# Prefix sums of a Mamba-2 block as split fp32r products, with every engine's order written anew

## What is computed

```
zxbcdt = hidden_states @ W_in
z, xBC, dt = jnp.split(zxbcdt, [D_INNER, D_INNER + CONV_DIM], axis=-1)
dt = jax.nn.softplus(dt + dt_bias)
xBC = jax.nn.silu(_causal_conv(xBC, conv_w, conv_b))
a = -jnp.exp(A_log)
y = _ssd(x * dt[..., None], dt * a, B, C)
y = y + x * D[None, None, :, None]
y = y * jax.nn.silu(z)
y = y * jax.lax.rsqrt(jnp.mean(y * y, axis=-1, keepdims=True) + EPS) * rms_w
out = y @ W_out          # then residual and a second layer norm
```

## Time and profile before

| | |
|---|---|
| runs (us) | 782.20, 781.74, 781.94 |
| the profiled execution | 780.59 us, span 778.9 us |
| TensorE clock granted, mean | 0.993 |
| busy: PE, PEld | 748.7 us (96%), 626.4 us (80%) |
| busy: DVE, ACT, POOL | 716.5 us (92%), 675.0 us (87%), 646.7 us (83%) |
| DMA | 20.14 MB, mean 26 GB/s |

### The profile page before, as it was taken

How to read it: one execution, slowest core, us unless ns; L and a number is a source line. 1 busy time by engine, 2 the same in 40 slices (tenths; PEclk the granted TensorE clock), 3 DMA queues, 4 the chain that set the end, 5 groups by cost and what they waited for, 6 DMA issues and landing times. The chain is left out here.

```text
span 778.9 us, 19524 instructions
## 1 busy us (share of the span) xinstructions
PE 748.7 (96%) x5412; PEld 626.4 (80%) x5412; DVE 716.5 (92%) x1594; ACT 675.0 (87%) x1716; POOL 646.7 (83%) x1220
## 2 busy tenths in 40 slices
PE   7799999999999999999999999999999999999983
PEld 6667788878888888888888888888888888888863
DVE  3689899999999999999999999999999999999885
ACT  4988899988898998899898889899889998888873
POOL 5577888988888888888898888888888889887774
PEclk8999999999999999999999999999999999999998
DMA  6000100000000000000000000000000000000000
GB/s 198 2 14 8 35 29 29 15 29 27 13 27 27 17 23 27 15 25 27 27 13 27 27 13 27 27 22 19 27 15 25 27 27 13 27 13 13 1 28 27
DMA packets 21418, 20.14 MB, mean 26 GB/s; under 512 B 2832, under 2 KB 20880, under 8 KB 21392
## 3 DMA queue, kind: packets, MB, share of 16 engines
q1 hardware_dynamic: 20176, 19.82, 7.6%
q10 hardware_dynamic: 1216, 0.02, 0.1%
HBM read 11.45 MB, written 8.39 MB: 25 GB/s over the span
## 5 line engine op out<-in xcount | busy, mean ns | idle before, releaser
L825 DVE SCALAR_TENSOR_TENSOR u<-ring,cw,u 128x256 f32<-128x256 f32 x558 | 260.4, 477 | 9.5 <-ACT u L1393 1.7
L1719 PE MATMUL ring<-xhl,wh 128*128 128x262 f32 x744 | 166.0, 315 | 1.0
L1719 PE MATMUL ring<-wh,xhl 128*128 128x512 f32 (+1 forms) x512 | 158.6, 370 | 1.5 <-DVE u L825 1.0
L1393 ACT ACTIVATE u<-ring,cb,cw 128x256 f32<-128x256 f32 x186 | 106.1, 571 | 51.6 <-PE ring L1719 48.2
L1719 PEld LDWEIGHTS ring<-xhl,wh 128*128 128x128 f32 x744 | 118.4, 189 | 34.5 <-DVE u L825 20.6
L1453 ACT ACTIVATE xdt<-xt_bank,dts 128x64 f32<-128x64 f32 x512 | 111.4, 332 | 0.5 <-PE xt_bank L1799 0.5
L1719 PE MATMUL ring<-xhl,wl 128*128 128x262 f32 x372 | 105.6, 284 | 0.0
L1719 PEld LDWEIGHTS ring<-wh,xhl 128*128 128x128 f32 x512 | 90.1, 188 | 19.3 <-issue 5.1
L847 DVE SCALAR_TENSOR_TENSOR lay<-e_bank,btg 128x512 f32<-128x512 f32 x128 | 87.8, 686 | 15.3 <-ACT e_bank L1436 11.9
L1719 PE MATMUL ring<-wl,xhl 128*128 128x264 f32 (+1 forms) x256 | 86.8, 339 | 0.0
L1436 ACT ACTIVATE e_bank<-e_bank 128x512 f32<-128x512 f32 x128 | 75.4, 589 | 5.7 <-PE e_bank L1824 5.1
(11 more groups left out here) (189 smaller groups left out, 2119.9 us busy)
## 6 DMA issues: line engine op xcount, KB each, us to landing
xin<-in_x_dram SPq DMA_DIRECT2D x32, 256.0 KB, 2.7
out_dram<-obuf SPq DMA_DIRECT2D x31, 256.0 KB, 2.2
lay<-in_w_in_dram SPq DMA_DIRECT2D x1, 776.0 KB, 4.7
lay<-in_w_in_dram SPq DMA_DIRECT2D x1, 512.0 KB, 9.3
wo<-in_w_out_dram SPq DMA_DIRECT2D x1, 512.0 KB, 6.1
lay<-in_f2t_dram SPq DMA_DIRECT2D x1, 256.0 KB, 6.3
lay<-in_f_dram SPq DMA_DIRECT2D x1, 256.0 KB, 8.3
lay<-in_f1t_dram SPq DMA_DIRECT2D x1, 256.0 KB, 8.6
```

Source lines behind the costliest of these rows:

```text
L825: v.scalar_tensor_tensor(out=u[:, ct], in0=conv_bank(k, ct)[:, :, t:t + P], scalar=cw[:, ct, t:t + 1], in1=u[:, ct], op0=ALU.mult, op1=ALU ...
L1393: s.activation(u[:, ct], conv_bank(k, ct)[:, :, HALO:PH], ACT.Identity, bias=cb[:, ct:ct + 1], scale=cw[:, ct, HALO:TAPS]).then_inc(u_done ...
L1719: last = mul(out, a, c, start=first and i == 0, stop=i == n - 1)
```

## The change

1. dt*a is made in three POOL operations in place of one: `a_exact` (128x16), its fp32r copy `a_high` (128x4x16), and the rest `a_low` (same shape). Softplus has steps 0 to 13 and not 0 to 11. ACT's `x_times_dt` waits for dt itself (softplus step 10) and not for the last step.
2. `sums` is six fp32r matmuls in place of three fp32 ones: each of the three products is done with the high and then the low part, added in PSUM. Four POOL operations of 128x128 in the head make the fp32r triangles and the constant columns.
3. `exp_a` moves on ACT from the very front to behind the weight splits, the first branch and five convolution blocks.
4. The order of calls is new on PE, DVE, ACT and POOL, in head, loop and tail. In the loop most of it is a rotation (where the loop turns around), but some calls really move, as shown below.

```diff
-SOFT_STEPS = 2 * LOG_TERMS + 2
+SOFT_STEPS = 2 * LOG_TERMS + 4
...
+            def split_constants():
+                pool.wait_ge(s_gp, 36)
+                g.tensor_copy(upto_r[:, :], upto[:, :])
+                g.tensor_copy(after_r[:, :], after[:, :])
+                g.tensor_copy(a_high[:, :], a_wide[:, :])
+                g.tensor_scalar(a_low[:, :], a_wide[:, :], 0.0, None, ALU.mult).then_inc(s_const, 1)
...
-                        pool.wait_ge(s_an, 2)
-                    shape = [P, QUAD, Q * H]
-                    wide = a_wide[:, :].rearrange("p (r n) -> p r n", r=QUAD)[:, :, 0:Q * H]
-                    g.tensor_tensor(wide, dts[:, b].unsqueeze(1).to_broadcast(shape),
-                                    a_neg[:, :].unsqueeze(1).to_broadcast(shape), ALU.mult).then_inc(a_done, 1)
+                    if i == 2 * LOG_TERMS + 1:
+                        if begun(k - 1):
+                            pool.wait_ge(a_done, k)
+                        else:
+                            pool.wait_ge(s_an, 2)
+                        g.tensor_tensor(a_exact[:, :], dts[:, b], a_neg[:, :], ALU.mult).then_inc(soft, 1)
+                    elif i == 2 * LOG_TERMS + 2:
+                        if begun(k - 1):
+                            pool.wait_ge(sums_in_psum, k)
+                        else:
+                            pool.wait_ge(s_const, 2)
+                        apart(pool)
+                        g.tensor_copy(high, spread).then_inc(soft, 1)
                     else:
+                        g.tensor_tensor(low, spread, high.bitcast(F32), ALU.subtract).then_inc(a_done, 1)
                     return
...
-                act.wait_ge(a_done, k + 1)
+                act.wait_ge(soft, (SOFT_STEPS - 1) * k + 2 * LOG_TERMS + 1)
...
-                mul(bg_bank[:, 0:n], upto[:, :], a_wide[:, 0:n], start=True, stop=True)
-                mul(bg_bank[:, n:2 * n], after[:, :], a_wide[:, 0:n], start=True, stop=True)
-                mul(bg_bank[:, 64:64 + P], a_wide[:, :], upto[:, :], start=True, stop=True).then_inc(sums_in_psum, 1)
+                for part, (first_part, last_part) in ((a_high, (True, False)), (a_low, (False, True))):
+                    mul(bg_bank[:, 0:n], upto_r[:, :], part[:, 0:n], start=first_part, stop=last_part)
+                for part, (first_part, last_part) in ((a_high, (True, False)), (a_low, (False, True))):
+                    mul(bg_bank[:, n:2 * n], after_r[:, :], part[:, 0:n], start=first_part, stop=last_part)
+                for part, (first_part, last_part) in ((a_high, (True, False)), (a_low, (False, True))):
+                    last = mul(bg_bank[:, 64:64 + P], part[:, :], upto_r[:, :], start=first_part, stop=last_part)
+                last.then_inc(sums_in_psum, 1)
...
             def head():
                 small_loads()
-                exp_a()
                 norm_apply(0, 0)
```

More of the change, by code:

```diff
@@ L160, in program @@
         a_wide = sb("a_wide", [P, P])
+        a_exact = sb("a_exact", [P, Q * H])
+        a_high = sb("a_high", [P, P], F32R)
+        a_low = sb("a_low", [P, P], F32R)
+        upto_r = sb("upto_r", [P, P], F32R)
+        after_r = sb("after_r", [P, P], F32R)
         rows = sb("rows", [P, P], F32R)
@@ new lines, in head @@
+                mask_g(2, 1)
+                scale_x(2, 2, 1)
+                softplus(3, 0, 9)
+                softplus(3, 0, 10)
+                softplus(3, 0, 11)
+                softplus(3, 0, 12)
+                rms_scale(1)
+                softplus(3, 0, 13)
+                decay_state(2, 2, 0)
+                residual_bias(2, 2)
+                decay_state(2, 2, 1)
+                state_weights(3, 0)
+                layer_norm_scale(4)
+                decay_state(3, 0, 0)
+                spread_rows(3)
@@ new lines, in head @@
+                scale_x(3, 0, 0)
+                residual(3, 0)
+                mask_g(3, 0)
+                last_norm_scale(1)
+                skip_x(3, 0, 0)
+                skip_x(2, 2, 1)
+                output(1, 1)
+                softplus(4, 1, 0)
+                softplus(4, 1, 1)
+                softplus(4, 1, 2)
+                softplus(4, 1, 3)
+                softplus(4, 1, 4)
+                softplus(4, 1, 5)
+                softplus(4, 1, 6)
+                softplus(4, 1, 7)
@@ L983, in one_pass @@
                 b1, b2, bo = (b + 1) % BUF, (b + 2) % BUF, (b - 1) % BUF
+                if live(k - 2):
+                    add_diag(k - 2, 1)
                 if live(k):
+                    tap(k, 2, 0)
+                    tap(k, 2, 1)
+                if live(k - 2):
+                    apply_gate(k - 2, b1, 1)
+                if live(k):
+                    tap(k, 2, 2)
+                    tap(k, 0, 0)
+                    tap(k, 0, 1)
+                    tap(k, 0, 2)
+                if live(k - 1):
+                    weigh(k - 1, 1, 0)
+                if live(k - 2):
+                    last_h(k - 2, b1, 0)
+                if live(k):
+                    tap(k, 3, 0)
+                    tap(k, 3, 1)
+                    tap(k, 3, 2)
+                    tap(k, 1, 0)
+                    tap(k, 1, 1)
                     tap(k, 1, 2)
+                if live(k - 2):
+                    y_low(k - 2, 1)
+                if live(k):
+                    low_rows(k)
                 if live(k - 1):
@@ L1121, in head @@
                 tap(1, 1, 2)
-                new_state(0, 0)
-                low_rows(1)
-                y_skip(0, 0)
+                weigh(0, 1, 0)
+                norm_stats(3, 0)
                 tap(1, 4, 0)
@@ L1538, in head @@
+                branch(0)
                 conv_in(0, 3)
[L1539 to L1544 removed]
+                softplus_exp(0)
+                first_table()
+                softplus_den(0)
+                conv_in(0, 5)
+                exp_a()
+                norm_apply(1, 1)
+                z_silu(0, 0, 0)
+                left_table(2)
                 conv_in(0, 0)
[L1546 removed]
```

769 lines of the change are left out of this document (361 added, 408 removed).

## The result

The changed kernel takes 804.7 us (median of 802.91, 804.73, 805.01 and 804.72) where the kernel before took 781.8 us beside it: a ratio of 1.0277, interval 1.0263 to 1.0291. It is slower by 2.8%; forecast were 782.1 us, with a range up to 787.5. The profiled execution is the one of 802.91 us, with a span of 801.2 us.

A forecast was written before the change was run, and what follows sets the result against it. PE's work was put at about 22.8 us a pass plus 0.2 waiting; POOL would become the bound. 780.59 + 0 (PE) + 1.9 (POOL) - 2 (head) + 0.25 (tail) = 780.7, as median 782.1 us; range 776 to 787.5.

The forecast's parts named there:

- POOL needs 23.00 - 0.63 = 22.37 us a pass, and has 0.63 us to spare: POOL in the loop: its wait of `output` for ACT's `last_apply`, 0.63 us a pass, was counted as spare time.
- the 0.63 us go. POOL's pass is then 22.37 + 0.7 = 23.07 us: POOL in the loop: the wait vanishes, 0.7 us is added, and POOL becomes the bound, 0.07 us a pass above before.
- Sums on PE, cost 0: Sums on PE: six fp32r matmuls at 0.11 us each take 0.66 us, like the three fp32 products, so nothing is saved.
- POOL's own addition, 0.7 us: dt*a on POOL: three operations take 1.14 us where 0.45 us was counted before, 0.7 us a pass more.
- `output`'s wait goes: POOL in the loop: a 1.0 us state decay ahead of `output` removes its 0.63 us a pass wait for ACT.
- PE waits for a_low in most passes: Sums on PE: the sign that POOL is the bound, at 23.0 to 23.15 us a pass.
- PE's wait for taps goes: Block 4 on PE: its tap comes some 1.0 us earlier on DVE, so the 0.2 us a pass wait goes.
- the relief: Rival, chance 0.25: POOL stays under 22.8 us a pass, block 4's 0.2 us wait is won, PE decides: 774.8 us.
- ACT's new places are hidden by its 10% of free time: ACT in the loop: the moved `z_silu`, `square` and `decay` cost nothing.
- The late scale: Rival, chance 0.25: `last_norm_scale` on POOL ends 1.4 us later, `y_diag` on PE stands 0.2 to 0.3 us a pass: 787.0 us.
- Head -2: Head: earlier xn and better order against later first sums; bounds -4 to +1 us, taken as -2 us.
- Tail +0.25: Tail: `residual_bias(n0)` between the two `end_scale` delays the second by 0.25 us; other moves, -1 to +1, taken as 0.

The follow-up runs named there:

- The fills: Kernel before plus one POOL fill of an unread tile in each loop pass, behind last_norm_scale or behind a_wide: 795.51 and 796.33 us.
- e1: Kernel before with only the split arithmetic (three POOL operations, six fp32r products), all old orders kept: 803.77 us, ratio 1.0283.
- r1: Changed kernel with one POOL operation writing a_high, a_low left zero, six fp32r products kept: 791.03 us, ratio 1.0116 to the kernel before.
- e2: Changed kernel with its new orders, but one POOL operation a_wide and three fp32 products: 790.18 us, ratio 1.0105 to the kernel before.
- s2: e2 with ACT's loop alone put back to its old order: 799.88 us, ratio 1.0228 to the kernel before.
- c1: e1 with a_exact, a_high and a_low made by DVE in the loop and not by POOL: 798.19 us, ratio 1.0208 to the kernel before.

## Why the prediction was wrong

The step that failed is "POOL needs 23.00 - 0.63 = 22.37 us a pass, and has 0.63 us to spare", and with it "the 0.63 us go. POOL's pass is then 22.37 + 0.7 = 23.07 us". The fills put what POOL could spare at 0.13 us. With the split at 0.7 us that alone makes 0.57 us a pass, or 15 us; e1, which has nothing else, lost 0.67 us a pass. Even there POOL still waits for ACT, 9.4 us in 16 times or 0.39 a pass: the wait came along and was never room.

- **Sums on PE, cost 0:** right. 0.72 us and r1 equal to e2. The Trainium skill's page FP8 and Floating Point Precision, section TensorE Precision Notes, has true fp32 as four passes; the estimate by that rule was 0.33 us a step saved. The changed trace does not show that, with 0.72 us for 0.67, as the row of before had said.
- **POOL's own addition, 0.7 us:** right. In e1 (POOL, two passes) the three take (427.98 - 427.25) + (404.73 - 404.45) = 1.01 us from start to next start, against 0.27, so 0.74 (a_low of one pass and the step behind it, then the three of the next pass):

```profile
404.45 0.32 POOL L501 TENSOR_TENSOR a_low<-a_exact,a_high 128x64 fp32r<-128x64 f32 x1
404.73 0.70 POOL L561 TENSOR_TENSOR rr<-ss,nhalf 128x2 f32<-128x2 f32 x1
...
427.25 0.22 POOL L492 TENSOR_TENSOR a_exact<-dts,a_neg 128x16 f32<-128x16 f32 x1
427.67 0.24 POOL L499 CAST a_high<-a_exact 128x64 fp32r<-128x64 f32 x1 [0.19 <-POOL a_exact L492]
427.98 0.32 POOL L501 TENSOR_TENSOR a_low<-a_exact,a_high 128x64 fp32r<-128x64 f32 x1
```

- **`output`'s wait goes:** half. It fell from 15.7 to 7.8 us with a 1.04 us decay in it. In the pass shown ACT starts `last_apply` only when the late scale ends, and POOL waits 0.49 us for it behind the decay.
- **PE waits for a_low in most passes (the sign of POOL as the bound):** no. It does so 10 times, 4.8 us in all. The lost time reaches PE by several other waits as well.
- **PE's wait for taps goes:** half. Block 4's is gone in the pass read here: it starts 0.23 us behind z's last product. But z itself, which comes earlier since `y_tokens` has left its place, now waits 0.49 us for taps in each of the three passes read, which the prediction did not look at (the loading of weights first, then PE):

```profile
404.41 0.19 PEld L1751 LDWEIGHTS ring<-wh,xhl 128*128 128x128 f32 x1 [0.49 <-DVE u L857]
```

```profile
405.75 0.40 PE L1751 MATMUL ring<-wh,xhl 128*128 128x512 f32 x1
405.98 0.40 PE L1751 MATMUL ring<-xhl,wh 128*128 128x262 f32 x2
```

  In all the wait fell from 19.7 to 12.1 us; in e2, with the same orders but no split, it is 22.7 us in 50 times, 0.87 at z and 0.20 at block 4 in one pass. So the 0.2 us a pass of the relief were not won.
- **ACT's new places are hidden by its 10% of free time:** open. ACT waits 0.57 us for the scale in the pass shown, 0.48 a pass for the squares and 0.62 for xn, so its free time is spent in waits. But its old order beside the other new ones is slower still (s2), and no run prices these places alone.
- **The late scale, 0.25 us a pass, chance 0.25:** its signs all came. The scale was forecast to end 12.2 + 1.4 = 13.6 us behind the sums, and ended 416.81 - 402.96 = 13.85 behind. PE was to stand 0.2 to 0.3 us a pass and stands 0.26. The pass is longer than its 23.25 us, and its 787.0 us are far off, since it took the 0.63 us as spare like the rest. But it is not the cause by itself: e2's trace has no wait of `last_apply` for the scale among its longest, and its pass is 0.23 us longer nevertheless; and with the split POOL is late itself, which delays the scale as well. How much of the 0.42 us goes by this path no run tells. That 0.23 equals the rival's price is chance, as far as the runs tell.
- **Head -2:** wrong, +3.1 by the fifth sums, of which 0.65 is a loop pass (traces of a head differ by 1.5 us and more). The transposes at 8.53 us (8.3 forecast) and `f_inner` at 10.87 (10.8) came as worked out. But the first softplus on POOL started at 24.25 and not at 24.72, so 0.5 us was left of the 1.2 expected, and with the residual ahead of the split the first sums came at 30.4 and not at 29.0.
- **Tail +0.25:** +1.0, within the bounds of -1 to +1 on top of it.

The range failed by the loop: head and tail as measured would have moved 782.1 us only to 787.3. The bounds of 776 to 787.5 never priced "POOL has nothing to spare", 0.7 us x 27 = 19 us, or 781.9 + 19 = 801, an estimate from the row of POOL. The view showed a wait, I read it as slack, and put no rival beside that reading.

## What to carry to other kernels

A wait before one instruction is at most slack for that instruction: what is queued ahead of it on the same engine has readers of its own, and each must be looked up before the wait is spent. A cheap probe tells it: a fill of known length in the loop, at the place in question; if it costs its length, nothing was free. Orders written for four engines at once are one object: putting one engine's list back made it slower in every case, with PE's and POOL's by more than the whole change did.

## What the runs showed of the hardware

- fp32r products with 128 weight columns and only 16 or 128 columns streamed start 0.11 to 0.14 us apart at the full granted clock (changed kernel, at 403 us), as fast as the two records of an fp32 product.
- The three operations of the split last 0.22, 0.24 and 0.32 us on POOL and cost 1.01 us from start to next start (e1), with 0.19 us of idle time ahead of a_high, which reads the result just before it. On DVE (c1) they last 0.17, 0.19 and 0.21 us:

```profile
L870 DVE TENSOR_TENSOR a_exact<-dts,a_neg x4: 165/166/168, 117.7 to 188.0; 128x16 f32<-128x16 f32 x4
L874 DVE CAST a_high<-a_exact x4: 184/187/189, 118.2 to 188.5; 128x64 fp32r<-128x64 f32 x4
L877 DVE TENSOR_TENSOR a_low<-a_exact,a_high x4: 213/215/215, 118.7 to 189.0; 128x64 fp32r<-128x64 f32 x4
```
